# Null-key attention on one core: the value products of two rounds put one behind the other in every second round

## The reference, cut to what matters

```python
q = split_heads(x_normed @ Wq) * 64 ** -0.5        # 16 heads, 256 queries a batch
k, v = split(context @ Wkv)                        # 256 keys a batch, 512 features in
k = concat(null_key, k);  v = concat(null_value, v)    # 257 keys
attn = softmax(q @ k.T)
out = (attn @ v) @ Wout                            # 1024 -> 256 features
x = x + layernorm(out)
```

## The kernel before

| r | place 0 | place 1 | place 2 |
|---|---|---|---|
| 0 | | query front | key front |
| 1 | | null | query front |
| 2 | query front | project | key front |
| 3 | | key front | |
| 4 | | query front | key front |
| 5 | | value front | |
| 6 | | value front | value front |
| 7 | | value front | |

## Time and profile before

### The profile page before, as it was taken

One profiled execution on the slowest core, in us unless ns is written; L12 is line 12 of the kernel. 1 busy time (PEld: TensorE's weight loads), 2 busy tenths in 40 slices (PEclk: granted clock), 3 DMA queues, 4 the chain that ended last, 5 costly groups with the idle time before them and its releaser, 6 DMA issues. The chain is left out here.

```text
span 2502.6 us, 38309 instructions
## 1 busy us (share of the span) xinstructions
PE 2104.7 (84%) x14693; PEld 1560.5 (62%) x14693; DVE 1269.5 (51%) x2527; ACT 1006.7 (40%) x2844; POOL 273.0 (11%) x357
## 2 busy tenths in 40 slices
PE   6868788799997689689999999969998987874884
PEld 4545555566665479656666666557876766653673
DVE  5446665688886244445544445654435445451003
ACT  3235555577776145223333333442223443332212
POOL 0100000122121424200000000040001000002004
PEclk8979999999999899899999999989999999996986
DMA  3000000112122622330000000010011000021432
GB/s 124 18 1 1 1 1 14 48 36 55 40 51 68 229 69 72 100 128 9 9 9 9 1 9 1 1 30 1 1 49 43 18 9 20 1 87 69 163 99 72
DMA packets 87873, 110.53 MB, mean 44 GB/s; under 512 B 18088, under 2 KB 71344, under 8 KB 86800
## 3 DMA queue, kind: packets, MB, share of 16 engines
q1 hardware_dynamic: 82752, 94.52, 12.3%
q0 software_dynamic: 4944, 13.57, 1.6%
HBM read 77.77 MB, written 22.95 MB: 40 GB/s over the span
## 5 line engine op out<-in xcount | busy, mean ns | idle before, releaser
L898 ACT ACTIVATE ca_prob<-bank,ca_nmax 128x512 f32<-128x512 f32 x256 | 174.0, 690 | 74.7 <-DVE ca_nmax L965 74.7
L898 ACT ACTIVATE na_prob<-bank,na_nmax 128x257 f32<-128x257 f32 x256 | 118.0, 474 | 206.6 <-DVE na_nmax L965 206.6
L965 DVE TENSOR_REDUCE ca_nmax<-bank 128x1 f32<-128x512 f32 x256 | 163.9, 682 | 41.6 <-PE bank L755 41.6
L898 ACT ACTIVATE ra_prob<-bank,ra_nmax 128x256 f32<-128x256 f32 x256 | 118.2, 482 | 105.6 <-DVE ra_nmax L965 105.6
L769 PE MATMUL bank<-cst,ca_prob 128*128 128x128 f32 x1024 | 141.9, 280 | 6.8 <-DVE ca_pT L971 5.2
L769 PEld LDWEIGHTS bank<-cst,ca_prob 128*128 128x128 f32 x1024 | 112.2, 142 | 52.7 <-issue 44.4
L965 DVE TENSOR_REDUCE na_nmax<-bank 128x1 f32<-128x257 f32 x256 | 90.8, 417 | 82.6 <-PE bank L755 82.6
L2116 PE MATMUL bank<-sf_h,sf_W 128*128 128x512 f32 x512 | 120.4, 395 | 0.3 <-DVE sf_h L2188 0.3
L2010 PE MATMUL bank<-na_Wkv,na_cxT 128*128 128x512 f32 x256 | 115.4, 595 | 0.0
L2116 PEld LDWEIGHTS bank<-sf_h,sf_W 128*128 128x128 f32 x512 | 95.8, 187 | 24.3 <-DVE sf_h L2188 1.0
L2159 ACT ACTIVATE ln_sq<-bank,sf_sc 128x512 f32<-128x512 f32 x64 | 43.8, 690 | 130.3 <-PE bank L2116 119.9
(11 more groups left out here) (464 smaller groups left out, 4627.6 us busy)
## 6 DMA issues: line engine op xcount, KB each, us to landing
xl_w<-in_L_ffn_w SPq DMA_DIRECT2D x16, 1024.0 KB, 7.5
rf_sent<-rf_w SPq DMA_DIRECT2D x13, 390.0 KB, 6.2
rf_xin<-rf_sent SPq DMA_DIRECT2D x39, 128.0 KB
dp_cx<-in_ctx_tok SPq DMA_DIRECT2D x4, 1024.0 KB, 14.4
ca_v<-in_ctx_values SPq DMA_DIRECT2D x8, 512.0 KB, 4.7
rf_W<-in_L_ffn_w SPq DMA_DIRECT2D x8, 512.0 KB
rf_rows<-rf_back SPq DMA_DIRECT2D x8, 512.0 KB
na_Wkv<-in_L_xattn_Wkv SPq DMA_DIRECT2D x1, 4096.0 KB, 16.1
```

Of the source, the lines that this page charges most:

```text
L898: e = act.activation(prob[:, n % 2, u, hh * keys:(hh + 1) * keys], S[u][:, hh * keys:(hh + 1) * keys], ACT.Exp, bias=nmax[:, n % 2, u, hh: ...
L965: v.tensor_reduce(nmax[:, n % 2, u], S[u][:, 0:W].rearrange("p (h k) -> p h k", h=per), AX.X, ALU.max, negate=True).then_inc(maxed, 1)
```

## The change

In the null attention alone (`pairs=True`), value products are no longer issued in every round. In every odd iteration n, values(n-3) and values(n-2) are issued one behind the other, in the place where values(n-2) stood; even iterations have none. Since the turned probabilities then live for one round longer, `pT` gets three buffers instead of two. The number of instructions on each engine stays the same.

```diff
-                     divide=False, made=lambda b, k: False):
+                     divide=False, pairs=False, made=lambda b, k: False):
...
-    pT = sb("pT", [P, 2, GA * NB, 2, P])
+
+    PT = 3 if pairs else 2
+    pT = sb("pT", [P, PT, GA * NB, 2, P])
...
     def values_due(n):
-        return 2 <= n <= NR + 1 and (n - 2) % VR == VR - 1
+        every = 2 if pairs else VR
+        return 2 <= n <= NR + 1 and (n - 2) % every == every - 1
...
+            def values_of(n):
+                if pairs:
+                    values((n - 2) // VR - 1)
+                values((n - 2) // VR)
+
...
-                                p = pT[:, w % 2, a * NB + hh * KC + c].rearrange("p i q -> p (i q)")
+                                p = pT[:, w % PT, a * NB + hh * KC + c].rearrange("p i q -> p (i q)")
...
                     if values_due(n):
-                        values((n - 2) // VR)
+                        values_of(n)
...
-                o = pT[:, n // 2 % 2, 4 * f:4 * f + 4, n % 2] if GA == 4 else pT[:, n % 2, :, f]
+                o = pT[:, n // 2 % 2, 4 * f:4 * f + 4, n % 2] if GA == 4 else pT[:, n % PT, :, f]
...
-                             null={"values": nv, "out": Wo}, divide=True, made=lambda b, k: b < 2 and k in (1, 3, 5, 7))
+                             null={"values": nv, "out": Wo}, divide=True, pairs=True, made=lambda b, k: b < 2 and k in (1, 3, 5, 7))
```

## The result

| | before | after |
|---|---|---|
| median | 2503.58 us (9 runs, 2494.54 to 2507.60) | 2517.92 us (9 runs, 2512.19 to 2520.39) |
| ratio to before, 95% interval | | 1.0057 (1.0042 to 1.0071) |
| profiled execution, its span | 2504.42, 2502.6 us | 2512.33, 2510.5 us |

The change made the kernel 0.6% slower: 14.3 us by the medians, where 15.2 were forecast. Of the changed kernel's profile, the busy time by stretch comes first (length, busy PE, PEld, DVE, ACT, POOL, granted clock, DMA): the null attention from its first scores to its last projection product, the rest of the program behind it, then batches 0 and 7.

The account below looks back on a forecast made before the run. PE's instruction list was taken to bound six of eight batches. Six batches at +2.53 us (+15.2), batch 0 +1.0 and batch 7 -1.0 sum to +15.2; 2501.05 + 15.2 gives 2516 us, range 2506 to 2524.

Parts of the forecast that it names:

- The pair of value groups: Odd iterations of the null attention: a second group running on behind the first adds 0.86 us on PE.
- a fresh start for each group: Rival on joined value groups: each costs 1.01 in place of 0.86 us, +4 us, 2520; no chance given.
- weight loads that don't overlap: Rival on the second value group: each pair takes a matmul's full 0.38 us, 18 us more, 2534; chance 0.02.
- The even rounds: Batches 1 to 6, value group removed: gains 0.00 at r = 0 and 4, 0.17 at r = 2, 0.16 at r = 6.
- The second value front: Round r = 6: released by DVE's copy, it can start at 1358.39 in place of 1358.55, gaining 0.16 us.
- The odd rounds: Batches 1 to 6: r = 3, 5 and 7 each pay 0.86 us, r = 1 pays 0.28.
- The wait of the query front for ACT's null columns: Round r = 1: the 0.50 us wait goes, since two value groups cover ACT's copy.
- Batch 0: First batch: n = 5 pays 0.32, n = 6 gives 0.16, n = 7 pays 0.86, together +1.0 us.
- Batch 7: Last batch: net -0.6 us behind the projection, -0.36 behind the last turn, together -1.0.
- M's copy doesn't bind: Rival on the shared bank: second fronts start once PE is free, the removal pays in full, -14.6 us, 2486; chance 0.04.
- The clock: Rival on new PE waits at r = 0 and 4: key fronts run at 1.2 GHz, 40 us more, 2556; chance 0.02.
- The case of no measurable difference: Rival on the whole kernel: right mechanism, but a difference within 0.5% (12.5 us); chance 0.26.

Follow-up runs that it names:

- experiments 2 to 4: Experiment 2, experiment 3, and a fourth: kernel before with the query fronts of r = 0 and r = 4 copied by ACT, ratio 0.9993.
- Experiment 2: Kernel before, no pairs, with the value group of even iterations issued behind the last shared use instead of between the two; ratio 1.0098, batch 74.09 us.
- experiment 3: Changed kernel with the query fronts of r = 0 and r = 4 copied out of M by ACT instead of DVE; ratio 1.0034, batch 71.72 us.
- Experiment 5: Changed kernel with, in even iterations with two shared uses, the first ahead of the turn and the second behind it; ratio 0.9979, batch 69.42 us.
- experiment 7: Changed kernel with the first of two fronts ahead of the turn, and value groups one by one in r = 2 and 3; 2489.07 us, ratio 0.9952.
- experiment 1: Changed kernel with the third pT buffer kept but value groups back to one a round; ratio 0.9993 to the kernel before.

## Why the prediction was right, point by point

**Size and sign.** 2516 was forecast, in 2506 to 2524, and 2517.92 measured. The forecast stood on a median of before of 2501.05, and in the nine runs it was 2503.58; so the time came out 1.7 us higher than forecast and the difference 0.9 us smaller. The layer took 15.64 us more, where the sum was 15.2.

**The pair of value groups.** Forecast: the second group adds 0.86, at 0.215 a pair of matmuls. In the changed kernel's timeline a group of r = 3 and what follows it:

```profile
1418.33 1.49 PEld L801 LDWEIGHTS bank<-na_pT,na_v 128*64 128x64 f32 x16 [0.33 <-issue]
1418.33 1.95 PE L801 MATMUL bank<-na_pT,na_v 128*64 128x256 f32 x16
...
1420.21 1.14 PE L758 MATMUL bank<-na_k,na_q 64*128 64x257 f32 x8
```

1420.21 - 1418.33 = 1.88, against 1.01 to 1.02 for one group: 0.87. The rival of a fresh start for each group (1.01) falls, and so does that of weight loads that don't overlap: at the 0.38 us of a matmul for each pair a double group would last over 3 us, and the row of PEld shows the loads beside the matmuls. The Trainium skill ("TensorE: Matmul & The Clock Gate", Part 3) says that a weight load overlaps a matmul in flight only where it goes to another group of rows. The trace does not agree for these pairs, which all use the same 128 rows: eight of them and the step to the next product take 1.88 us.

**The even rounds.** r = 0 and 4 were to give nothing and gave -0.01 (8.83 against 8.82). r = 2 was to give 0.17 and gave 17.06 - 16.90 = 0.16. r = 6 was to give 0.16 and gave 10.17 - 10.02 = 0.15. Its rows are, before and after:

```profile
1422.35:1432.52 10.17, 10.17 (x43) 4.88 (x41) 4.65 (x12) 2.42 (x9) 0.19 (x1) 1.00 0.00 0
```
```profile
1436.44:1446.46 10.02, 9.23 (x35) 4.40 (x33) 4.65 (x12) 2.43 (x9) 0.19 (x1) 1.00 0.00 0
```

The second value front was to start 0.05 behind the end of DVE's copy and starts 0.06 behind it:

```profile
1442.08 0.69 DVE L2024 COPY na_v<-bank 128x512 f32<-128x512 f32 x1 [1.11 <-PE bank L2018]
...
1442.83 3.70 PE L2018 MATMUL bank<-na_Wkv,na_cxT 128*128 128x512 f32 x8 [0.79 <-DVE na_v L2024]
```

**The odd rounds.** r = 1 took 6.11 us against the 5.82 of before, +0.29 where 0.28 was forecast; r = 3 took 7.43 against 6.56, +0.87 where 0.86 was. In all a batch went from 70.34 to 72.92, +2.58 where 2.53 was forecast. The wait of the query front for ACT's null columns is gone, as forecast.

**The ends.** Batch 0, from first scores to first scores, went from 1157.73 - 1113.65 = 44.08 to 45.32 us, +1.24 where +1.0 was forecast. Here a term was too small. In iteration 5 the start of the value front was to gain 0.54 us on the first scores of the layer; it gained 0.42 (22.82 to 22.40), and with a front 0.10 longer only 0.32 was left of it. That is the 0.2 by which the forecast of batch 0 was short. PE's row before, then the rows after:

```profile
1136.47 3.60 PE L2010 MATMUL bank<-na_Wkv,na_cxT 128*128 128x512 f32 x8
```
```profile
1138.19 1.18 PE L772 MATMUL bank<-cst,na_prob 128*128 128x128 f32 x8
1138.57 0.68 DVE L2000 TENSOR_SCALAR na_q<-bank 128x512 f32<-128x512 f32 x1
...
1139.30 0.30 PEld L2018 LDWEIGHTS bank<-na_Wkv,na_cxT 128*128 128x128 f32 x2 [0.18 <-DVE na_q L2000]
1139.31 3.70 PE L2018 MATMUL bank<-na_Wkv,na_cxT 128*128 128x512 f32 x8
```

The value front starts 1139.31 - (1138.57 + 0.68) = 0.06 us behind DVE's copy of the queries. That is the same wait for M on which the prediction rests, and in this iteration its sum left the wait out. Batch 7 went from 1630.85 - 1579.73 = 51.12 to 50.07, -1.05 where -1.0 was forecast. Both parts came near: up to the first scores of its last round it went from 33.06 to 32.35 us (-0.7 where -0.6 was forecast), from there on from 18.06 to 17.72 (-0.34 where -0.36 was).

**The rivals.** That M's copy doesn't bind fell with the waits of 1.29 us and with experiments 2 to 4. The clock stayed at 1.00 in the whole layer, with idle time of 1.29 us twice a batch. The case of no measurable difference did not come, as the whole interval lies above 1. But it was near: the interval is 10.5 to 17.8 us, so that the difference exceeds the 12.5 us which the prediction took as its bound is not shown. That the bank's copy and not the pairing is the cause was argued in the prediction from the trace alone. Experiment 2 shows it without pairs, and experiment 3 moves the wait by moving what it waits for. Experiment 5 takes it away from r = 0, 4 and 6, and experiment 7 from r = 2 as well.

## What to carry to other kernels

When several products share one PSUM bank, look at what the busy engine does between two of them before you move it: work in another bank there is cover for the copy, though the trace shows hardly any wait (0.26 us here stood for a cover of 1.0). Joining groups saves only the start of a group (0.15 us each here), while taking cover away gives nothing back until the copy has ended (0.00 us for a group of 1.01 at r = 0), so find other cover first (here the turn, with the copy ahead of the division) and join only where it exists. An engine's share of busy time can fall while the time grows, and the place to read the cost is the distance between two starts in the round that was to get shorter.

## What the runs showed of the hardware

The two heads' value products write different halves of the partitions, and the instructions of a group start two at a time, 0.006 us apart, with a new pair every 0.215 us. Which two make a pair the trace does not name. Two groups with met waits between them run on at that pace. The first product behind a group of another kind comes later: 0.31 us behind the last start, where products of its own kind follow each other at 0.22. A product that waits for a bank starts 0.05 to 0.06 us after the copy out of it ends, on DVE and on ACT alike. Unexpected was how much the unchanged rest of the program varies: behind the layer the nine profiled executions, one of each kernel, took from 860.75 to 873.36 us for the same work, at mean granted clocks of PE from 0.93 (860.75) down to 0.91 (873.36). The layer, at clock 1.00 throughout, repeats to some hundredths (517.20 and 517.24 us in the kernel before and in experiment 1). How the lowered clock comes to fall differently there was not tried.
